# Causal attention of a two-layer decoder: masks written by row strips, loops of four slots, the split of the maxima on GpSimd

## The reference, cut to what matters

```
x        : (64, 128, 128)                    # batches, tokens, features
xn       = layernorm(x)
q, k, v  = xn @ Wq, xn @ Wk, xn @ Wv         # Wq = W_dq W_uq, and so on; 16 heads of 8 lanes
s        = q k^T / sqrt(8), per head, with keys later than the query masked (-1e30)
x        = x + softmax(s) v @ W_o
```

## Time and profile before

| | us |
|---|---|
| median of 3 runs (3176.43 to 3181.77) | 3179.05 |
| the profiled execution | 3173.24 |
| its span, first to last instruction | 3171.5 |
| granted TensorE clock, mean | 0.958 |
| self-attention of layer 0: first transpose of xn to last x + y | 31.0 to 512.0 |

### The profile page before, as it was taken

One profiled execution on the slowest core, in us unless ns is written; L12 is line 12 of the kernel. 1 busy time (PEld: TensorE's weight loads), 2 busy tenths in 40 slices (PEclk: granted clock), 3 DMA queues, 4 the chain that ended last, 5 costly groups with the idle time before them and its releaser, 6 DMA issues. The chain is left out here.

```text
span 3171.5 us, 79074 instructions
## 1 busy us (share of the span) xinstructions
PE 2810.4 (89%) x26182; PEld 2315.9 (73%) x26183; DVE 2213.5 (70%) x4747; ACT 1914.9 (60%) x4303; POOL 1819.8 (57%) x2990
## 2 busy tenths in 40 slices
PE   6999997999999999499995999996789999999996
PEld 4666675888888888387774777774467777777775
DVE  4877885667666676445553999996878787878643
ACT  2555553666666666354442667674677777777762
POOL 3333333556666666425556777773667777777752
PEclk9999998999999999699997999997699999999998
DMA  5555563000000000122222000000000000000000
GB/s 151 156 143 157 157 169 107 2 5 13 14 11 13 13 12 15 68 69 74 74 74 68 1 0 0 0 0 1 1 1 5 8 5 8 5 8 5 8 5 10
DMA packets 205118, 129.51 MB, mean 41 GB/s; under 512 B 14256, under 2 KB 197528, under 8 KB 204184
## 3 DMA queue, kind: packets, MB, share of 16 engines
q1 hardware_dynamic: 196632, 108.60, 12.1%
q0 software_dynamic: 8192, 16.79, 1.7%
HBM read 34.85 MB, written 90.51 MB: 40 GB/s over the span
## 5 line engine op out<-in xcount | busy, mean ns | idle before, releaser
L445 ACT ACTIVATE a_e<-a_ps_s 128x512 f32<-128x512 f32 x256 | 138.9, 595 | 216.9 <-PE a_ps_s L371 216.9
L1575 POOL TENSOR_TENSOR a_qk<-a_qkv 128x2048 f32<-128x2048 f32 x64 | 235.3, 3676 | 57.8 <-ACT a_qkv L1550 53.6
L1508 PE MATMUL a_ps_s<-a_qk,w_ident 128*128 128x256 f32 x1024 | 236.7, 385 | 26.5 <-POOL a_qk L1575 26.4
L988 POOL TENSOR_TENSOR x_p<-x_p,x_rz 128x1232 f32<-128x1232 f32 x64 | 143.9, 2248 | 170.4 <-DVE x_rz L1097 170.4
L1508 PEld LDWEIGHTS a_ps_s<-a_qk,w_ident 128*128 128x128 f32 x1024 | 192.1, 192 | 55.9 <-issue 22.4
L524 POOL TENSOR_TENSOR a_k_bd<-a_kT,w_block 128x512 f32<-128x512 f32 x64 | 67.1, 1050 | 280.2 <-ACT a_kT L476 280.2
L1366 POOL DMA_INDIRECT f_yg<-f_rows_out,f_index x128 | 122.8, 959 | 177.7 <-DVE f_yo L1446 159.3
L547 DVE TENSOR_REDUCE a_nmax<-a_ps_s 128x4 f32<-128x512 f32 x256 | 164.0, 682 | 84.3 <-PE a_ps_s L366 84.3
L1557 ACT ACTIVATE a_r<-a_o,w_a_rows 128x128 f32<-128x128 f32 x512 | 220.8, 522 | 2.1 <-DVE a_o L1607 2.1
L2224 POOL TENSOR_TENSOR x_sq<-x_e 128x1232 f32<-128x1232 f32 x64 | 143.3, 2240 | 127.4 <-DVE x_t_sq L2383 127.3
L1104 DVE TENSOR_REDUCE x_top<-x_ps_s 128x16 f32<-128x1232 f32 x64 | 91.2, 1425 | 110.3 <-PE x_ps_s L728 110.3
(11 more groups left out here) (588 smaller groups left out, 9755.6 us busy)
## 6 DMA issues: line engine op xcount, KB each, us to landing
f_rows_in<-a_zeros SPq DMA_DIRECT2D x31, 1088.0 KB, 5.4
f_rows_out<-a_zeros SPq DMA_DIRECT2D x31, 1088.0 KB, 10.2
f_xin<-f_rows_in SPq DMA_DIRECT2D x135, 64.0 KB
f_rows_out<-f_yo SPq DMA_DIRECT2D x135, 64.0 KB
out<-x SPq DMA_DIRECT2D x16, 256.0 KB
f_raw<-in_late_f SPq DMA_DIRECT2D x2, 1408.0 KB, 6.1
w_ctx<-in_ctx SPq DMA_DIRECT2D x1, 2464.0 KB
f_rows_in<-f_xr,f_where POOLq DMA_INDIRECT x128
```

What stands on the lines that cost most here:

```text
L988: nc.gpsimd.tensor_tensor(wide, wide, rz[:, :].unsqueeze(2).broadcast_to([P, HEADS, K]), ALU.mult).then_inc(p_ready, 1)
L1508: ins = nc.tensor.matmul(ps_s[u % 2][:, 0:HEADS * HEADS], c.ident[:, :], qk[:, u % 2, k, :, :], start=k == 0, stop=k == HD - 1)
L1575: nc.gpsimd.tensor_tensor(qk[:, u % 2, :, :, :], qkv[:, u, 0, :, :].unsqueeze(3).broadcast_to(full), qkv[:, u, 1, :, :].unsqueeze(2).broad ...
```

## The change: what it does

- The masks. A causal mask of 128x128 is cut into a coarse part (whole 32x32 tiles that are masked) and the triangles on the four diagonal tiles. The coarse part of the natural scores is one matmul of a single row strip per bank (`coarse_q`, `coarse_k`); that of the turned scores lies in extra rows of `pad` and `m_bd` and comes in with the shift matmul. The triangles are four matmuls of one row strip and 4x32 columns per bank (`causal_tiles`). The four full-height mask matmuls of a half are gone.
- PE waits for both maxima (or both exponentials) of a bank pair at once, and does so ahead of the shift matmuls.
- `run_slots` has a body of four slots on PE, ACT and DVE; POOL stays at eight. The rings of q, k_bd, xT and v1 have four places.
- The split of the maxima into three bf16 parts goes from DVE to POOL, ahead of `k_bd` in the slot. `nmax` has two places.
- On DVE the maxima of pair 1 come after `o`; x + y and both statistics come last.
- On PE, `y` goes from the second tail to the first, one slot later; the transpose of `o` goes from the first tail to the second; v is projected two slots after q and k. AHEAD is 12.
- Five constant tiles become one (`a0_rows16`) and a small one.

```diff
-        AHEAD = 11
+        AHEAD = 12
...
         @block.tensor
         def _(pe):
-            def masked(bank, mask):
-                nc.tensor.matmul(bank[:, :].rearrange("p (t k) -> p t k", t=GROUP), c.ident16[:, :],
-                                 mask[:, :].unsqueeze(1).broadcast_to([P, GROUP, P]), start=True, stop=False)
+            def causal_tiles(g, tri, n):
+
+                nc.tensor.matmul(ps_s[g].rearrange("p (t k) -> p t k", t=GROUP)[:, :, n * STRIP:n * STRIP + STRIP], c.place16[strip(g), n, :],
+                                 tri[strip(g), :].unsqueeze(1).broadcast_to([STRIP, GROUP, STRIP]), start=False, stop=False)
 
...
-                    for n, g in enumerate(PAIRS[pair]):
-                        if sl.fixed and s < 3 - pair:
-                            wait(pe, max_done[pair], 2 * s - 1 + n)
-                        else:
-                            pe.wait_ge(exp_done[pair], 2 * (s - 2 + pair) - 1 + n)
-                        masked(ps_s[g], c.mask_q)
+                    if sl.fixed and s < 3 - pair:
+                        wait(pe, max_done[pair], 2 * s)
+                    else:
+                        pe.wait_ge(exp_done[pair], 2 * (s - 2 + pair))
+                    for g in PAIRS[pair]:
+                        nc.tensor.matmul(ps_s[g][:, :].rearrange("p (t k) -> p t k", t=GROUP), c.coarse_q[strip(g), :],
+                                         c.coarse_k[strip(g), :].unsqueeze(1).broadcast_to([STRIP, GROUP, P]), start=True, stop=False)
                 if weighed:
                     s, u = weighed
-                    for n, g in enumerate(PAIRS[other]):
-                        pe.wait_ge(max_done[other], 2 * upto(sl, s + 2 + pair) - 1 + n)
-                        if sl.fixed and s + 2 + pair > B:
-                            pe.wait_ge(exp_done[other], 2 * s - 1 + n)
-                        masked(ps_s[g], c.mask_k)
                     pe.wait_ge(shift_ready, s + 1)
+                    pe.wait_ge(max_done[other], 2 * upto(sl, s + 2 + pair))
+                    if sl.fixed and s + 2 + pair > B:
+                        pe.wait_ge(exp_done[other], 2 * s)
                     for g in PAIRS[other]:
-                        nc.tensor.matmul(ps_s[g][:, :], c.ones16[strip(g), :], m_bd[strip(g), u % 2, :, :], start=False, stop=False)
+                        nc.tensor.matmul(ps_s[g][:, :], c.shift16[strip(g), :], m_bd[strip(g), u % 2, :, :], start=True, stop=False)
+                for n in range(GROUPS):
+                    if scored:
+                        for g in PAIRS[pair]:
+                            causal_tiles(g, c.tri_q, n)
+                    if weighed:
+                        for g in PAIRS[other]:
+                            causal_tiles(g, c.tri_k, n)
...
+                if at := sl.step(ADD):
+                    s, u = at
+                    pe.wait_ge(oT_ready, s + 1)
+                    wait(pe, x_done, s)
+                    wait(pe, shift_ready, upto(sl, s + ADD - SHIFT))
+                    nc.tensor.matmul(ps_y, oT[:, :], c.w["a0_o"][:, :], start=True, stop=True).then_inc(y_ps, 1)
                 if at := sl.step(SHIFT):
                     s, u = at
                     pe.wait_ge(pad_ready, s + 1)
                     wait(pe, shift_ready, s)
-                    wait(pe, o_ready, s + SHIFT - VALUE)
+                    wait(pe, x_done, s + SHIFT - ADD)
                     nc.tensor.transpose(ps_pad, pad[:, u % 2, :, :].rearrange("p h r -> p (h r)"), c.ident16[:, :]).then_inc(pad_ps, 1)
+                half(sl, 1)
                 if at := sl.step(LAST):
...
+                if at := sl.step(SCORE):
+                    s, u = at
+                    wait(pe, v_ready, s)
+                    wait(pe, q_ready, upto(sl, s + SCORE - PROJECT))
+                    wait(pe, xT_ready, upto(sl, s + SCORE - TURN))
+                    nc.tensor.matmul(ps_qkvx[:, 2 * P:3 * P], xT[:, u, :], c.a0_v[:, :], start=True, stop=True).then_inc(v_ps, 1)
...
-                if at := sl.step(LAST):
-                    s, u = at
-                    pe.wait_ge(oT_ready, s + 1)
-                    wait(pe, x_done, s)
-                    nc.tensor.matmul(ps_y[:, 0:P], oT[:, :], c.w["a0_o"][:, :], start=True, stop=True).then_inc(y_ps, 1)
+                    wait(pe, q_ready, s)
+                    wait(pe, v_ready, s + PROJECT - SCORE)
+                    nc.tensor.matmul(ps_qkvx[:, P:2 * P], c.a0_k[:, :], xT[:, u, :], start=True, stop=True)
+                    nc.tensor.matmul(ps_qkvx[:, 0:P], c.a0_q[:, :], xT[:, u, :], start=True, stop=True).then_inc(qk_ps, 1)
...
-            run_slots(pe, slot, B, LAG, RING)
+            run_slots(pe, slot, B, LAG)
...
+                if at := sl.step(LAST):
+                    s, u = at
+                    act.wait_ge(oT_ps, s + 1)
+                    wait(act, y_ps, s)
+                    nc.scalar.activation(oT[:, :], ps_last, ACT.Copy).then_inc(oT_ready, 1)
...
+                if at := sl.step(SCORE):
+                    s, u = at
+                    pool.wait_ge(max_done[0], 2 * s + 2)
+                    pool.wait_ge(max_done[1], 2 * s + 2)
+                    wait(pool, pad_ps, s - 1)
+                    left = nmax[:, u % 2, :, :].rearrange("p g t -> p (g t)")
+                    for n in range(2):
+                        part = pad[:, u % 2, :, n]
+                        nc.gpsimd.tensor_tensor(part, left, ones[:, :], ALU.mult).then_inc(own, 1)
+                        pool.wait_ge(own, 4 * s + 2 * n + 1)
+                        nc.gpsimd.tensor_tensor(rest[:, n, :], left, part, ALU.subtract).then_inc(own, 1)
+                        pool.wait_ge(own, 4 * s + 2 * n + 2)
+                        left = rest[:, n, :]
+                    nc.gpsimd.tensor_tensor(pad[:, u % 2, :, 2], left, ones[:, :], ALU.mult).then_inc(pad_ready, 1)
+                if at := sl.step(PROJECT):
+                    s, u = at
+                    pool.wait_ge(k_ready, s + 1)
+                    wait(pool, sT_ps[0], s - 3)
+                    wait(pool, sT_ps[1], s - 3)
+                    nc.gpsimd.tensor_tensor(k_bd[:, u % UNROLL, :, :], kT[:, u % 2, :].unsqueeze(1).broadcast_to([P, GROUP, P]),
+                                            c.block[:, 0:GROUP].unsqueeze(2).broadcast_to([P, GROUP, P]),
+                                            ALU.mult).then_inc(bd_ready, 1)
...
-                if scored:
-                    maxima(scored, 1)
-                    s, u = scored
-                    wait(dve, pad_ps, s - 1)
-                    for pair in range(2):
-                        dve.wait_ge(max_done[pair], 2 * s + 2)
-                    left = nmax[:, :, :].rearrange("p g t -> p (g t)")
-                    for n in range(2):
-                        part = pad[:, u % 2, :, n]
-                        nc.vector.tensor_copy(part, left).then_inc(own, 1)
-                        dve.wait_ge(own, 4 * s + 2 * n + 1)
-                        nc.vector.tensor_tensor(rest[:, n, :], left, part, ALU.subtract).then_inc(own, 1)
-                        dve.wait_ge(own, 4 * s + 2 * n + 2)
-                        left = rest[:, n, :]
-                    nc.vector.tensor_copy(pad[:, u % 2, :, 2], left).then_inc(pad_ready, 1)
-                if at := sl.step(VALUE):
+                if at := sl.step(LAST):
...
+                if scored:
+                    maxima(scored, 1)
+                if at := sl.step(ADD):
+                    s, u = at
+                    dve.wait_ge(y_ps, s + 1)
+                    nc.vector.tensor_tensor(c.x[:, s, :], c.x[:, s, :], ps_y, ALU.add).then_inc(x_done, 1)
...
-            run_slots(dve, slot, B, LAG, RING)
+            run_slots(dve, slot, B, LAG)
```

More of the change, by code:

```diff
@@ L283, in self_attention @@
         xn = sb("xn", [P, 2, D])
-        xT = sb("xT", [P, 2, P])
-        q, kT = sb("q", [P, 4, P]), sb("kT", [P, 2, P])
-        k_bd = sb("k_bd", [P, 4, GROUP, P])
-        v1 = sb("v1", [P, RING, HEADS, WIDE])
+        xT = sb("xT", [P, UNROLL, P])
+        q, kT = sb("q", [P, UNROLL, P]), sb("kT", [P, 2, P])
+        k_bd = sb("k_bd", [P, UNROLL, GROUP, P])
+        v1 = sb("v1", [P, UNROLL, HEADS, WIDE])
         zeros = sb("zeros", [P, D])
-        nmax = sb("nmax", [P, GROUPS, GROUP])
-        rest = sb("rest", [P, 2, HEADS])
+        nmax = sb("nmax", [P, 2, GROUPS, GROUP])
+        ones, rest = sb("ones", [P, HEADS]), sb("rest", [P, 2, HEADS])
         pad = sb("pad", [P, 2, HEADS, HD], BF16)
@@ L365, in half @@
                         for g in PAIRS[pair]:
-                            nat = nc.tensor.matmul(ps_s[g][:, j * P:j * P + P], q[strip(g), u % 4, :], k_bd[strip(g), u % 4, j, :],
+                            nat = nc.tensor.matmul(ps_s[g][:, j * P:j * P + P], q[strip(g), u, :], k_bd[strip(g), u, j, :],
                                                    start=False, stop=j == GROUP - 1)
@@ L370, in half @@
                         for g in PAIRS[other]:
```

(30 more changed lines are left out.)

96 lines of the change are left out of this document (39 added, 57 removed).

## The result

| | before | changed |
|---|---|---|
| median, us | 3178.53 (3176.43 to 3181.77, 4 runs) | 3127.20 (3125.51 to 3128.01, 4 runs) |
| the profiled execution | 3173.24 | 3127.54 |
| span, granted clock | 3171.5, 0.958 | 3125.8, 0.955 |

The ratio is 0.9836 [0.982, 0.9852]: 51 us less, where 74 less had been forecast. The time lies inside the range, and the sign is right; a third of the expected gain is missing.

The account below looks back on a forecast made before the run. PE was taken to bound the self-attention slots, with DVE close behind. Slots -54, jumps -18 and start -2 sum to -74 us: 3173.2 - 74 = 3099, with 5.8 for the median 3105 us; range 3072 to 3155.

Parts of the forecast that it names:

- Masks: PE's half in self-attention: full-height mask matmuls go, 16 small ones cost 0.40 us (0.22 to 0.86), so a half takes 1.61.
- The wait: PE ahead of the shift matmuls: waits for DVE's maxima, 1.37 us after leaving a half, with the tails filling this time.
- the fourth rival: DVE's maxima still trail, slot near 6.8 us, only jumps gained: 3150 us; 12% together with serial small matmuls.
- Slot: One self-attention slot: 2 x (1.37 + 1.61) = 5.96 us, taken as 6.12 against 6.975 before, 0.86 us gained.
- the 0.16 us that I left in: Slot before: 6.81 us from PE's timeline against a mean of 6.975; this difference was kept in the forecast, giving 6.12.
- The split on POOL: Split chain moved from DVE: 1.7 us on POOL, ready 1 us before PE wants `pad`; cost 0.
- The rival in which POOL is the bound: POOL's small instructions slow beside DVE, its slot takes 8.7 us: +88 us, 3267 us; chance 8%.
- Jumps: Loop jumps of PE: a body of 1192 matmuls and loads stays loaded, so the four jumps' 18.4 us go.
- the second rival: PE's loop body is fetched again at every jump; nine jumps lose 23 us: -33 us in all, 3146 us; chance 20%.
- Start: Kernel start: v1's first memset of 4.37 us halves with the ring, POOL's first scalars stand behind it: 2 us less.
- The step that failed: Self-attention stage: the slot's gain of 0.86 us applied to all 63 slots, 54 us.
- other moves: v two slots later, `o` earlier on DVE, one constant tile: cover of a slot or more, so 0 us.

## Why the prediction was right in sign and too large

*Masks, right, and slightly better.* A half was forecast at 1.61 us and takes 1.49. The 16 small matmuls cost 0.23 us, the lower bound of 0.22, not my 0.40: four strips do share the columns, and the 25 ns of the cross-attention's is no limit (here they start 14 ns apart). Triangles left out and doubled confirm it (0.46 and 0.45 us for 32). `y` in the first tail costs 0.33, not 0.22, so that tail is 1.49 instead of 1.31.

*The wait, right in length, half right in name.* The second tail with its wait is 1.55 us, where I had 1.37. I had put only DVE's maxima there; ACT's exponentials release the coarse matmuls 0.15 us before, and the trace names them in most waits (68 of PEld at L348, one wait of PE at L357 names the maxima). Without the split on POOL the maxima would trail, as the fourth rival has it: the experiment with the split on DVE shows that state.

*Slot, right within 0.10 us, in part by luck.* 6.02 us against 6.12 forecast, 0.96 instead of 0.86 saved, wherever PE's code is resident. The two halves came out 0.24 us under their terms and the two tails 0.30 over them, and the 0.16 us that I left in did not come.

*The split on POOL, right:* no PE wait, instructions of 0.23 to 0.27 us, 1.3 us to spare (1 forecast). The rival in which POOL is the bound fell.

*Jumps, right.* The 18 us came back: 1192 matmuls and loads stay, as do 1448; 1601 and 1936 don't. The trace doesn't agree with the rule of the Trainium skill, "Runtime: NRT & Kernel Launch", section "Instruction fetch mechanics": by its two-page window each of the nine jumps would fetch, and from 118 us on, behind the first of them, none does. (The prediction calls this case the second rival; it is the first of its list.) The prediction's other reading, that a fetched body of 1936 speaks against the 2048 instructions, does not hold: it counted matmuls and loads alone, and a body's waits and register instructions come on top. The 4.6 us of a jump, "2.81 us and a slow restart", were idle time and clock: behind three of the four jumps before, PE was granted 0.50 for a while, and behind the fourth, with 1.00, the slot was the shortest (10.28).

*Start:* 3 us instead of 2, by the first transpose of xn (31.0 and 28.0).

*The step that failed* is "The gain is 0.86 us a slot, 54 us over 63 slots". It multiplied the loop's slot by all 63. Of these 7 lie ahead of the loop and 16 behind it in straight code, where each block of instructions is used once, and 4 are the first pass. Before, such slots were no longer than the others (6.8 us in the mean behind the loop, so 0.86 was 0.2 too much there as well), at 6.975 us for 242 matmuls and loads; 298 in 6.02 us is 1.4 times that pace (49.5 a microsecond, not 35). Beside the clears, 165 GB/s in the mean, blocks then come up to 2 us late, and PE's clock falls behind some of the stops. Of the 20.7 us lost that is 11.9 behind the loop and 7.5 at its start; the rest are the first slots, in which the pipeline fills. It is shown from both sides: in straight code fetches without clears don't stall, clears without fetches don't, and with the two kept apart 22 to 26 us come back. I had asked of the loop what it fetches and never of the straight code, and had counted "other moves" as covered.

*A second, smaller one.* With a shorter stage the last pair of clears, which SP issues behind x + y, ends after the stage: +3 us at its end. Early clears remove it (0.96 us).

*Left open.* The profiled executions differ by another 8 us in stages whose code is the same. Those stages vary by as much among the other kernels (963 to 974 us the last), so I put it to scatter; that isn't shown. Why a block's packet starts late beside the clears (in which queue it waits) and how that depends on their rate was not measured either, nor why the clock falls behind some stops and not behind others of the same length.

## What to carry to other kernels

Count the matmuls and loads of a PE loop body against the largest seen to stay (here 1448, with the waits and register instructions of such a body on top) and let the loop run as far as the engine's own steps reach, beyond the other engines' loops. A gain found in a loop's slot holds for straight code only if its instructions can be fetched at the new pace: look at the instruction queue and at idle time with no releaser there, and put bulk DMA traffic beside resident loops, not beside straight PE code. Two edits that each buy little (0.9967 and 1.0016 here) can be the two halves of one gain.

## What the runs showed of the hardware that was not expected

- A body of 1448 matmuls and loads jumps back with no fetch, one of 1601 is loaded again in every pass; in these kernels the limit lies between.
- A jump back to a body that doesn't stay isn't a fixed cost: PE stood still for 2.48 to 2.81 us before, 2.50 with no clears near, and 4.03 to 5.38 beside clears at 277 to 284 GB/s. Behind most such jumps the granted clock is 0.50 for some microseconds (348.5 to 354.5 above).
- 16 bf16 matmuls of 32 rows and 128 columns on four strips in turn take 0.23 us, 14 ns apart.
- A stall of instruction fetch has no line of its own: it shows as "issue" before an arbitrary matmul, with q8 packets at the same time. Over all fourteen profiles there are 101 such stops of 0.9 us or more in this stage, and each ends 1.2 to 1.7 us after the end of a q8 packet.
